# Cross-attention kernel, narrow layers: the last key rows of two units transposed as one set, and the even unit's values split around the output projection

## What is computed

```python
q = (x or rmsnorm(x, w)) @ Wq          # 8 x 512 x (16 heads)
k, v = ctx @ Wk, ctx @ Wv              # 8 x 77 x (16 heads)
probs = softmax(q k^T * scale + bias)  # per head, 512 x 77
x = x + (probs @ v) @ Wo + bo
```

## Time and profile before

| | us |
|---|---|
| median of three runs | 2065.75 (2065.2 to 2066.01) |
| the profiled execution | 2066.7 |
| its span, first to last instruction | 2064.9 |
| TensorE busy | 2024.2 |
| Vector engine busy | 1398.2 |
| ScalarE busy | 966.0 |
| GpSimd busy | 649.5 |

### The profile page before, as it was taken

One profiled execution on the slowest core, in us unless ns is written; L12 is line 12 of the kernel. 1 busy time (PEld: TensorE's weight loads), 2 busy tenths in 40 slices (PEclk: granted clock), 3 DMA queues, 4 the chain that ended last, 5 costly groups with the idle time before them and its releaser, 6 DMA issues.

```text
span 2064.9 us, 31181 instructions
## 1 busy us (share of the span) xinstructions
PE 2024.2 (98%) x11482; PEld 1760.5 (85%) x11482; DVE 1398.2 (68%) x2408; ACT 966.0 (47%) x1814; POOL 649.5 (31%) x534
## 2 busy tenths in 40 slices
PE   8999999999999998999999999999999989999998
PEld 8999988888888887788888888888888877888887
DVE  5332365775577557788888676557755775888886
ACT  3222354544355354555555454345443553555553
POOL 1000043311232244454444431223122543444441
PEclk9999999999999999999999999999999999999999
DMA  7889742222122222343333332222221222333332
GB/s 196 183 176 200 191 97 67 68 65 79 51 72 71 70 71 74 89 107 100 87 98 94 101 96 68 72 60 67 66 79 52 72 77 81 74 92 92 88 72 84
DMA packets 262537, 191.02 MB, mean 93 GB/s; under 512 B 197522, under 2 KB 199986, under 8 KB 259826
## 3 DMA queue, kind: packets, MB, share of 16 engines
q1 hardware_dynamic: 262386, 189.03, 35.7%
HBM read 132.66 MB, written 56.26 MB: 91 GB/s over the span
## 4 chain that ended last, share of the span: by engine, by line
PE 48%; issue 30%; POOL 11%; DVE 6%; ACT 2%; DMA 1%; SPq 1%; POOLq 0%; DVEq 0%; ACTq 0%
PE acc_bank L877 6%; POOL prob L1311 6%; PE acc_bank L261 4%; PE t_bank L857 4%; PE acc_bank L263 4%; PE acc_bank L262 4%; PE q_bank L835 4%; PE q_bank L837 3%; PE q_bank L839 3%; PE ctx_bank L261 3%; PE ctx_bank L262 3%; PE ctx_bank L263 3%; POOL x_s L1286 3%; PE s_bank L261 2%; POOL rest L1320 2%
## 5 line engine op out<-in xcount | busy, mean ns | idle before, releaser
L1311 POOL TENSOR_TENSOR prob<-prob,rinv 128x1232 f32<-128x1232 f32 x128 | 288.3, 2252 | 1006.3 <-DVE rinv L1195 1006.2
L1053 ACT ACTIVATE q_s<-q_bank 128x512 fp32r<-128x512 f32 x192 | 114.7, 597 | 489.3 <-PE q_bank L839 486.2
L877 PE MATMUL acc_bank<-pT_s,vals_s 128*128 128x512 f32 x1024 | 337.8, 415 | 0.0
L835 PE MATMUL q_bank<-x_s,w_s 128*128 128x512 f32 x768 | 319.4, 416 | 0.0
L1153 DVE TENSOR_REDUCE mx<-s_bank 128x4 f32<-128x308 f32 x512 | 240.1, 469 | 108.6 <-PE s_bank L801 54.3
L837 PE MATMUL q_bank<-x_s,w_s 128*128 128x512 f32 x768 | 313.3, 408 | 0.0
L839 PE MATMUL q_bank<-x_s,w_s 128*128 128x512 f32 x768 | 313.1, 408 | 0.0
L261 PE MATMUL acc_bank<-o_s,w_s 128*128 128x512 f32 x752 | 300.4, 400 | 2.8 <-DVE o_s L1186 2.5
L263 PE MATMUL acc_bank<-o_s,w_s 128*128 128x512 f32 x752 | 293.6, 390 | 0.0
L262 PE MATMUL acc_bank<-o_s,w_s 128*128 128x512 f32 x752 | 293.1, 390 | 0.0
L1044 ACT ACTIVATE prob<-prob,rstd 128x308 f32<-128x308 f32 x256 | 140.7, 553 | 263.2 <-DVE prob L1157 238.0
(11 more groups left out here) (107 smaller groups left out, 4092.8 us busy)
## 6 DMA issues: line engine op xcount, KB each, us to landing
stream<-x_back SPq DMA_DIRECT2D x128, 256.0 KB, 2.6
x_front<-stream SPq DMA_DIRECT2D x96, 256.0 KB, 3.3
x_back<-stream SPq DMA_DIRECT2D x96, 256.0 KB, 4.0
kvw_raw<-kvw SPq DMA_DIRECT2D x17, 1024.0 KB, 8.4
k_scr<-k_out SPq DMA_DIRECT2D x36, 308.0 KB, 10.5
keys_s<-k_scr SPq DMA_DIRECT2D x128, 77.0 KB, 2.5
v_scr<-v_out SPq DMA_DIRECT2D x8, 1024.0 KB
vals_s<-v_scr SPq DMA_DIRECT2D x512, 6.5 KB
```

The costliest lines, as they stand in the source:

```text
L835: pe.matmul(out, w[0], x_now[0], start=k == 0, stop=False)
L877: mm = pe.matmul(out, w, pT_s[:, part], start=i == mine[0] and part == 2 * n and w is v[0], stop=i == mine[-1] and w is terms[-1][0] and p ...
L1311: pool.tensor_tensor(view, view, rinv[:, slot].unsqueeze(2).broadcast_to([P, TILES * GH, CTX]), ALU.mult).then_inc(p_norm, 1)
```

## The change

In a narrow layer, two units (2i and 2i+1) share one transposed set n = 2. GpSimd copies the last 64 columns of each, normalised, into a half of `rest` (a new copy in every narrow unit). Only the odd unit's step transposes them, 128 wide, between its sets 0 and 1; the even unit has the sets 0 and 1 alone. ScalarE copies the two halves to partitions 0 to 63 and 64 to 127, the Vector engine writes their rests into the other half of each tile. The even unit's last two value matmuls need that set, which is made one step later than before: in the step of its values they move behind the first projection chunk, or, where that step has no chunk or is "ahead" (`carried`), into the next step behind the first half of the queries. Its result is then split at the head of the next step (ScalarE) and behind the second score tile (Vector engine; behind the fourth where carried). The numbering follows: `plan.t` for the sets, `plan.ended` for the order in which results end. The odd unit's value rows are loaded 64 partitions further.

```diff
+    def split_values(self, u):
+        return 0 <= u < NU and kind(u).name == "B" and u % 2 == 0
+    def carried(self, u):
+        return self.split_values(u) and (self.ahead(u + 2) or not self.projections(u + 2))
+    def turns(self, u):
...
+        return (0, 1, TWICE) if kind(u).name == "A" else (0, TWICE, 1) if u % 2 else (0, 1)
+    def rest_turn(self, u):
+        return self.t[(u if kind(u).name == "A" else u | 1, TWICE)]
...
             def turn(u, n):
+                item = plan.t[(u, n)]
...
-                if n == TWICE and a:
-                    pe.wait_ge(p_gathered, plan.gathered(u))
+                if n == TWICE:
+                    pe.wait_ge(p_gathered, u + 1)
                 for t in range(TILES):
...
-                        rows, p = (P, rest[:, t]) if a else (64, prob[:, u % 2, t, SC - REST_B:SC])
-                    mm = pe.transpose(t_bank[(3 * u + n) % 2][0:rows, t * P:t * P + P], p, ident[:, :])
+                    p = rest[:, t] if n == TWICE else prob[:, u % 2, t, base:base + P]
+                    mm = pe.transpose(t_bank[item % 2][:, t * P:t * P + P], p, ident[:, :])
...
             (TensorE, narrow step)
                     run(q, half)
+                    if plan.carried(s - 3):
+                        run(v_before, 2)
                     run(scores(s, 2), 1)
...
                     run(v, 3)
                     turned(0)
                     run(q, half)
-                    run(v, 9)
-                    turned(1)
+                    run(v, 3 if behind else 9)
+                    late_turns = plan.turns(s - 1)[1:]
+                    turned(late_turns[0])
                     if plan.stats_at(s) is not None:
                         stats(plan.stats_at(s))
-                    turned(2)
-                    if not plan.ahead(s):
-                        for gb, m in plan.projections(s):
-                            project(gb, m)
+                    for n in late_turns[1:]:
+                        turned(n)
+                    if behind and not plan.carried(s - 2):
+                        projected(projections[:1])
+                        run(v, 2)
+                        projected(projections[1:])
+                    else:
+                        projected(projections)
                 elif s == NU:
-                    run(v, 9)
-                    for gb, m in plan.projections(s):
-                        project(gb, m)
-                    turned(0)
-                    turned(1)
-                    turned(2)
+                    run(v, 6)
+                    for n in plan.turns(s - 1):
+                        turned(n)
+                    projected(projections)
+                    run(v, 2)
                     finish((0, 1))
...
             (Vector engine, rest_t)
+                if n == TWICE:
                     for m in range(2):
...
+                        rows, hi, lo = (REST_A, 0, 64) if kind(u).name == "A" else (64, 64 * m, 64 - 64 * m)
+                        e = dve.tensor_tensor(pT_s[lo:lo + rows, 2 * n + m], t_bank[item % 2][64 * m:64 * m + rows, :],
+                                              pT_s[hi:hi + rows, 2 * n + m].bitcast(F32), ALU.subtract)
                     e.then_inc(t_lo, 1)
...
             (Vector engine, narrow step)
-                    if s < NU:
-                        for t in range(TILES):
+                    for t in range(TILES):
+                        if s < NU:
                             tile_scores(s, t)
+                        if t == (3 if plan.carried(s - 3) else 1) and plan.split_values(s - 3):
+                            rest_o(s - 3, 0)
...
             (GpSimd, normalise)
+                pool.wait_ge(p_norm, u + 1)
+                if u:
+                    pool.wait_ge(t_mm, plan.rest_read_before(u))
...
+                else:
+                    pool.tensor_copy(rest[:, :, 64 * slot:64 * slot + 64], prob[:, slot, :, SC - REST_B:SC])\
+                        .then_inc(p_gathered, 1)
```

More of the change, by code:

```diff
@@ L135, in __init__ @@
             projections = [("proj", gb, m) for gb, m in self.projections(s)]
-            if self.ahead(s):
-                acc += projections
-            if 0 <= s - 2 < NU:
-                acc += [("pv", s - 2, m) for m in range(kind(s - 2).Q)]
-            if not self.ahead(s):
-                acc += projections
+            values = [("pv", s - 2, m) for m in range(kind(s - 2).Q)] if 0 <= s - 2 < NU else []
+            acc += projections + values if self.ahead(s) else values + projections
+            first = len(projections) if self.ahead(s) else 1 if self.split_values(s - 2) else 0
+            if self.carried(s - 3):
+                ends.append(("pv", s - 3, 0))
+            now = [] if self.carried(s - 2) else values
+            ends += projections[:first] + now + projections[first:]
+            turns += [(s - 1, n) for n in self.turns(s - 1)]
         self.q = {item: n for n, item in enumerate(queries)}
         self.acc = {item: n for n, item in enumerate(acc)}
+        self.ended = {item: n + 1 for n, item in enumerate(ends)}
+        self.t = {item: n for n, item in enumerate(turns)}
         self.q_splits = {item: n for n, item in enumerate(i for i in queries if i[0] == "q")}
@@ L149, in late @@
         found = self.projections(s) if s >= 0 else []
-        return found[-1:] if s < NU and kind(s).name == "B" and not self.ahead(s) else []
+        return found[-1:] if not self.ahead(s) and (s < NU and kind(s).name == "B" or self.split_values(s - 2)) else []
     def ahead(self, s):
@@ L713, in load_vals @@
                     col = w * h % P
+                    if kind(u).name == "B" and blk == TWICE and u % 2:
+                        row = (row + 64) % P
                     sp.dma_start(vals[row:row + t1 - t0, blk, 0:last - first, col:col + w], src)\
@@ L775, in _ @@
                         store(gb, m)
+                if s == NU + 1:
+                    for gb, m in plan.late(NU):
+                        load_back(gb + 1, m)
             for m in range(XC):
@@ L1106, in weights @@
                         split_weights(n)
+                if plan.split_values(s - 3) and not plan.carried(s - 3):
+                    split_o(s - 3, 0)
                 if s < NU and kind(s).name == "A":
@@ L1246, in _ @@
                     if s >= 1 and not plan.rest_later(s - 1):
-                        rest_t(s - 1, TWICE)
+                        for n in late_turns[1:]:
+                            turned(n)
                     for gb, m in plan.projections(s):
-                        add_result(gb, m)
+                        if (gb, m) not in plan.late(s):
+                            add_result(gb, m)
                     if plan.stats_at(s) is not None:
```

123 lines of the change are left out of this document (69 added, 54 removed).

## The result

| | before | after |
|---|---|---|
| median, us (22 runs each) | 2066.18 (2064.86 to 2068.07) | 2069.86 (2068.02 to 2071.71) |
| ratio after/before | | 1.0017 [1.0011, 1.0023] |
| span of the profiled execution, us | 2064.9 | 2068.3 |

The changed kernel is slower by 3.5 us (2066.18 x 0.0017), less than the 0.2% that I had called the limit of what can be told, but with an interval that leaves 1 out. The forecast was +2.2 us (0.1%), within 0.2% of no change.

A forecast was written before the change was run, and what follows sets the result against it. TensorE's own stream was taken as the bound, Vector next. Savings and new waits summed to +1.0 and +1.2 us in the two narrow layers, together +2.2: median 2068.0, own range 2064 to 2071.5, overall range 2055 to 2075.

The forecast's parts named there:

- What is removed: Narrow layers, odd steps: one set of four 64-wide transposes goes per pair of units, saving 0.44 us a pair.
- The even step: Two value matmuls moved behind the chunk wait for Vector's shared halves: 0.31 us lost per even step, bounds 0 and 0.6.
- Shifted subtractions: Vector, even step: two subtractions with shifted partitions do not overlap, 0.70 us each, so the halves end at 10.15.
- The odd step: TensorE's three values wait for Vector's rest of the even result: 0.18 us lost per odd step, bounds 0 and 0.4.
- the first chunk: Odd steps with a batch's first chunk: its tenth matmul waits for the same step's result rest, 0.19 us lost.
- Steps without a chunk: Steps 35, 36 and 99, 100: Vector is the bound and has work moved or hidden; 0.6 us gained per layer.
- The end: Step 127 and the end, transposes before the chunk: net gain 0.2 us instead of 0.44.
- SP's queue and the value loads: DMA queue: value loads start at 943.5 instead of 942.08, x and key loads shift 1.5 us; costs nothing if it keeps up.
- Vector's order becomes the bound: Rival, value matmuls ending even steps: later rests cost TensorE as much; with 0.3 a pair +7.8, 2076; chance 0.17.
- The new waits do not arise: Rival, narrow steps: Vector is ahead or TensorE's loads go ahead, so 14.8 us go: 2051; chance 0.17.
- smaller even wait: Rival, even steps: shifted halves overlap, end 9.93, loss 0.1 instead of 0.31: 2062.8; chance 0.13.
- no time saved: Rival, TensorE: 64-wide sets are cheap and the widened one dear, cancelling the saving: 13 us more, 2081; chance 0.03.

The follow-up runs named there:

- Run 2: Changed kernel with one query matmul more ahead of the values in odd narrow steps, one less behind the transposes: 2067.23 us, ratio 1.0005.
- run 3: Changed kernel with Vector taking the result rest ahead of the query rest in odd steps with a first chunk: 2066.66 us, ratio 1.0002.
- run 5: Kernel before, third set of every narrow unit transposed 128 wide instead of 64, nothing shared (wrong result): 2065.9 us, ratio 0.9999.
- run 1: Changed kernel with Vector subtracting the two shared halves ahead of the query rest in even narrow steps with a chunk: 2065.09 us, ratio 0.9994.
- run 9: Changed kernel with an extra, unused 0.68 us Vector sum ahead of the query rest in even narrow steps: 2089.78 us, one time.
- run 4: Changed kernel with the three edits of run 1, Run 2 and run 3 together, no other edit: 2055.32 us, ratio 0.9948.
- Run 7: Changed kernel with GpSimd's copy behind the norm's root, not in front of it, in steps with statistics: 2069.95 us, ratio 1.0016.
- run 11: Kernel of run 1 with the query rest moved further ahead, in front of the sums of the probabilities: 2075.83 us, one time.

## Why the prediction was right, and where it was off

- **What is removed (0.44 a pair).** Right. Odd steps with a first chunk are 0.03 shorter in spite of 0.37 us of forecast new waits (forecast 0.07), the others 0.22 (forecast 0.26). Run 2, which fills the wait of the statistics steps, has them at 10.45, 0.46 below the kernel before; run 3 takes one of the two waits of the first-chunk steps away and gets 10.25.
- **The widening, costed at nothing.** Right, run 5.
- **The even step (+0.31).** Right: +0.29 to 0.30; the halves end at 10.13 where I had 10.15, and the weight-load term of 0.11 is there (0.57 against 0.46). Runs 1 and 9 show the cause: take the wait away and the step falls to 10.50, add 0.6 to Vector and it grows by 0.59.
- **Shifted subtractions held at 0.70.** Right: 1.39 for two, the next 0.03 behind their end. The rule of the Trainium skill ("VectorE: DVE Perf Modes", Two Vector instructions with no wait between them) agrees; in run 1 the same holds with the halves ahead of the query rest (940.53 to 941.92, next at 941.95).
- **The odd step (+0.18) and the first chunk (+0.19).** Right to 0.06: run 2 gets 0.24 back where I had 0.18, run 3 gets 0.18. But the 0.24 is made up otherwise than my term: the reload behind the values stays in run 2, and 0.13 come from the fourth tile's scores, which wait for the bank that Vector's second subtraction frees (ended 946.65, scores 946.70) and for which I had no term. I had written that both waits add up in the first-chunk steps; run 2 alone gains nothing there, the three orders of run 4 together 0.35.
- **Steps without a chunk (-0.6 per layer).** The step that failed: +0.23 and +0.22 in the traces. It had named Vector as the bound there and priced Vector's instructions only. These terms came out in size: Vector starts step 35 0.58 later (forecast +0.5, as one more subtraction; in the trace it is the wait for ScalarE's halves) and takes 0.81 back in step 35 (forecast 0.71), so that it reaches step 36 0.23 ahead. But there the chain goes on through GpSimd's root to ScalarE's exponentials, and the root comes 1.05 later: 0.60 by the same late start of step 35, which delays the product ahead of the root before anything is taken back, and 0.45 by the copy that I costed at nothing "in an engine 47% busy". The root's lateness turns the 0.23 ahead into 0.51 behind, 0.74 of the 0.83 us between forecast and trace. Run 7 gets 0.34 of it back by moving the copy; the part of the product is read from the traces, no run takes it away. Two layers of this are 1.65 us, more than the whole difference between forecast and result (+2.2 against +3.5).
- **The end (-0.2 in layer 3)** came out at +0.1. The last odd step of layer 1 gave 0.51 for 0.4. In layer 1 three steps of the trace before that were 0.35 us too long hide 1.05 us of the loss. This part is luck: without it the traces would stand 4.5 us apart, twice the forecast's +2.2, though still inside its range.
- **SP's queue and the value loads:** nothing, right for the time, but not for the reason. The value loads of unit 44 are issued from 944.23 on (942.08 before), and the x loads queued behind do land late: ScalarE waits for them 14 times, 10.5 us in all (3 times and 0.8 before), most of it in first-chunk steps. I had named Vector or TensorE as the one that would wait. It costs nothing that shows: those steps take 10.42 to 10.44 whether the wait is 0.17 or 1.05.
- **The rivals.** "Vector's order becomes the bound" named the right place and the wrong size: the kernel after stands exactly on that edge (run 9 answers one to one: 0.59 for an instruction of 0.68, which delays the halves by some 0.6). "The new waits do not arise" (2051) comes within 4 us of what run 4 reached (2055.3), by reordering. The "smaller even wait" and "no time saved" fell to 10.13 and to run 5.

The forecast of the pairs came out (+2.05 per layer, +2.2 measured) because it priced an edit of order by the moment at which each result is there, not by the instructions that went. That the total came as near as it did owes something to two errors against each other, the steps without a chunk (1.65 us too low) and the three long steps of the kernel before (1.05 us that no term foresaw).

## What to carry to other kernels

Before work is taken from the busiest in-order engine, write down when each of its inputs is finished and put the helpers' work in the order in which the shortened stream asks for it: here the same instructions gave 2069.9 in the first order and 2055.3 in the second, against 2066.2 before (about 1 us of that in two steps, 33 and 97, where the kernel before had the same to gain). In this kernel a wait cost its own length and about 0.1 us more for the weight load that could not run ahead, so a result that is late by nothing at all still cost something (0.07, run 11); look for that in the distances of starts and in the idle time before weight loads. Sharing a piece between two units also bunches its after-work in one of them, and an engine that is far from busy on average (GpSimd, 33%) can still stand in the one chain that ends a stage.

## What had not been expected of the hardware

- Waits of 0.15 us leave no idle time of TensorE in the profile, since a modelled matmul (0.39) outlasts the distance to the next (0.23) by 0.16: TensorE was *busy* for 2.0 us more with 128 transposes fewer. Of a wait of 0.74 it shows 0.58 (run 9). The weight loads show the short ones (10.9 us before L906).
- A result that arrives when its matmul is due but after its weight load could have run costs 0.07 us for a score matmul of 308 columns (0.21 instead of 0.14 to the next, runs 1 and 11), and 0.11 for one of 512 behind a short wait (0.34 instead of 0.23, step 45 of the kernel after).
- 128-wide and 64-wide fp32 transposes cost the same in a row: 256 of them widened changed 2066.1 to 2065.9.
